# Pre-norm transposes reordered from token-major to feature-major, and the variance-row copies alternated between ScalarE and VectorE

## The reference, cut to what matters

```python
def _layernorm(x, axis=-1, eps=1e-5):
    m = jnp.mean(x, axis=axis, keepdims=True)
    v = jnp.var(x, axis=axis, keepdims=True)
    return (x - m) / jnp.sqrt(v + eps)

# x: (16, 2048, 1024); every sub-block is x + LN(f(LN(x)))
x = x + _layernorm(_L0_attn_ref(_layernorm(x), Wq, Wk, Wv, Wo))
x = x + _layernorm(_L0_ffn_ref(_layernorm(x), W_r, W_k, W_v, mu_r, mu_k))
x = x + _layernorm(_L1_attn_ref(_layernorm(x), W_attn, W_k2, W_proj))
x = x + _layernorm(_L1_ffn_ref(_layernorm(x), weights, scale, bias))

# _L0_attn_ref: 16 heads of 64; scores are a covariance plus a product of variances
qc = q - q.mean(axis=-1, keepdims=True)
kc = k - k.mean(axis=-1, keepdims=True)
cov = jnp.einsum('bhsd,bhtd->bhst', qc, kc) / D
q_var = jnp.var(q, axis=-1, ddof=1)
k_var = jnp.var(k, axis=-1, ddof=1)
scores = cov + q_var[..., :, None] * k_var[..., None, :] / D
out = softmax(scores) @ v          # then @ Wo
```

## Time and profile before

| | |
|---|---|
| median of 2 timed runs | 8365.75 us (8329.44 to 8402.06) |
| the profiled execution | 8285.25 us |
| its span on the slowest core (core 0) | 8283.6 us |
| spans of the other cores | 8252.1 to 8271.4 us |
| PE busy | 5208.9 us (63%) |
| DVE busy | 2943.7 us (36%) |
| ACT busy | 2610.7 us (32%) |
| PE, ACT, DVE on the chain that ended last | 44%, 10%, 22% |

### The profile page before, as it was taken

The page is one execution under the profiler, slowest core; times in us unless marked ns, Lnnn a source line. Parts: engine busy times, 40 slices in busy tenths (PEclk is TensorE's granted clock), DMA queues, the critical chain, the costliest instruction groups (busy, mean ns, idle before and its releaser), DMA issues.

```text
span 8283.6 us, 87354 instructions; the slowest of 8 cores (8252.1 to 8283.6 us)
## 1 busy us (share of the span) xinstructions
PE 5208.9 (63%) x27152; PEld 2902.5 (35%) x27392; DVE 2943.7 (36%) x4961; ACT 2610.7 (32%) x2875; POOL 375.8 (5%) x580
## 2 busy tenths in 40 slices
PE   4777777486466566654447777774865656666644
PEld 2444444233233333332124444442322333333321
DVE  3333332423433333335433333325134333333344
ACT  2443444110333333331024444441103333333310
POOL 0000000000000000000100000000000000000000
PEclk9777777698666666656667767766986666666566
DMA  2222222112122221111222222221121222111112
GB/s 36 18 18 22 21 18 15 13 16 21 5 12 12 14 12 11 7 10 11 52 32 18 18 25 18 18 17 11 16 21 5 12 13 13 11 11 7 10 11 49
DMA packets 244294, 140.02 MB, mean 17 GB/s; under 512 B 210946, under 2 KB 211074, under 8 KB 243842
## 3 DMA queue, kind: packets, MB, share of 16 engines
q1 hardware_dynamic: 21634, 33.72, 11.7%
q0 software_dynamic: 222208, 100.70, 9.1%
HBM read 117.59 MB, written 16.78 MB: 16 GB/s over the span
## 4 chain that ended last, share of the span: by engine, by line
PE 44%; DVE 22%; DMA 14%; ACT 10%; issue 9%; DVEq 1%; ACTq 0%; POOL 0%; SPq 0%; POOLq 0%
PE ps L114 24%; DMA TF<-TF 12%; PE psa L114 11%; PE psb L114 10%; ACT BCb L114 7%; DVE TF L114 7%; DVE STT L114 4%; DVE TBF L114 2%; DVE CH L114 2%; DVE WP L114 2%; ACT XT L114 1%; DVE XN L114 1%; DVE ODD L114 1%; DVEq L109 1%; DVE MV L114 1%
## 5 line engine op out<-in xcount | busy, mean ns | idle before, releaser
L114 ACT ACTIVATE BCb<-psa 128x1024 bf16<-128x1024 f32 (+1 forms) x1088 | 1059.1, 973 | 2297.0 <-PE psb L114 2177.0
L114 PE MATMUL ps<-BCb,VST 128*65 128x256 bf16 x6400 | 1262.9, 380 | 342.3 <-DVE BCb L114 319.4
L114 PEld LDWEIGHTS ps<-BCb,VST 128*65 128x65 bf16 x6400 | 1004.6, 161 | 596.8 <-issue 427.0
L114 DVE RECIPROCAL TF<-ps 1x512 f32<-1x512 f32 x256 | 858.0, 3352 | 958.7 <-PE psa L114 478.1
L114 ACT ACTIVATE BCb<-psb 128x1024 bf16<-128x1024 f32 (+1 forms) x1088 | 1054.7, 969 | 78.9 <-PE psb L114 62.0
L114 PE MATMUL ps<-XN,WP 128*128 128x512 bf16 x2936 | 861.3, 454 | 131.5 <-DVE CH L114 81.8
L114 PE MATMUL ps<-IDENTB,BA 128*128 128x128 bf16 x1024 | 129.4, 306 | 800.2 <-ACT BA L114 679.1
L114 PEld LDWEIGHTS ps<-XN,WP 128*128 128x128 bf16 x3072 | 344.8, 114 | 605.7 <-issue 406.9
L114 ACT ACT_TABLE_LOAD x43 | 55.2, 1283 | 1536.3 <-DVE SCR L114 845.2
L114 PE MATMUL psa<-QST,KST 65*128 65x256 bf16 x2048 | 369.3, 311 | 239.5 <-ACT BCb L114 190.5
L114 PE MATMUL psa<-XN,WP 128*128 128x512 bf16 (+1 forms) x1250 | 407.2, 408 | 126.6 <-DVE WP L114 108.3
(11 more groups left out here) (106 smaller groups left out, 5344.7 us busy)
## 6 DMA issues: line engine op xcount, KB each, us to landing
TF<-TF SPq DMA_DIRECT2D x256, 128.0 KB, 6.2
out<-X POOLq DMA_DIRECT2D x32, 512.0 KB, 5.6
X<-x POOLq DMA_DIRECT2D x32, 256.0 KB, 15.5
WP<-Wk POOLq DMA_DIRECT2D x32, 256.0 KB, 5.0
QST<-CH POOLq DMA_DIRECT2D x32, 256.0 KB, 2.9
KST<-CH POOLq DMA_DIRECT2D x32, 256.0 KB, 2.9
WP<-Wattn POOLq DMA_DIRECT2D x32, 256.0 KB, 4.7
WP<-Wq POOLq DMA_DIRECT2D x16, 256.0 KB, 4.5
```

Of the source, the lines that this page charges most:

```text
L114: instr = getattr(obj, rec["f"])(*rec["a"], **rec["k"])
```

## The change

Two edits.

1. `pre_ln`: the ACT normalisations stay in a loop over the 16 token tiles. The transposes and copies move out of it into a second loop, over the 8 feature chunks and, in each, two groups of 8 token tiles. A group transposes the block (tile, chunk) of 8 tiles into `PT`, and the copy moves the bank of 128x1024 to 1024 adjacent columns of one chunk of `XN`, and marks only that chunk as written. Counts and sizes of the ACT, PE and DVE instructions are as before (16 ACT, 128 transposes, 16 copies in each `pre_ln`).
2. `mk_sqvar`: the evacuations with even k stay on ACT, those with odd k become a DVE `tensor_copy` from the same bank to the same place. Banks, matmuls and DMAs are unchanged.

```diff
+            tiles = []
             for tt in range(TT):
...
+                tiles.append((dst_ap, dst_res))
                 b.op("s", "activation", dst_ap, X.t[:, tt * 1024: tt * 1024 + D],
...
-                ngrp = -(-C // 8)
-                for gi in range(ngrp):
-                    cs = list(range(gi * 8, min(C, gi * 8 + 8)))
-                    for k, c2 in enumerate(cs):
+            for c2 in range(C):
+                for g in range(-(-TT // 8)):
+                    ts = list(range(g * 8, min(TT, g * 8 + 8)))
+                    for k, tt in enumerate(ts):
+                        dst_ap, dst_res = tiles[tt]
                         b.op("t", "matmul", PT.t[:, k * 128:(k + 1) * 128],
                              dst_ap[:, c2 * 128:(c2 + 1) * 128], ident_ap,
-                             is_transpose=True, start=(k == 0), stop=(k == len(cs) - 1),
+                             is_transpose=True, start=(k == 0), stop=(k == len(ts) - 1),
                              r=list(dst_res) + IDENT.res, w=PT.res)
                     b.op("v", "tensor_copy",
-                         XNv[:, gi * 8: gi * 8 + len(cs), tt * 128: tt * 128 + 128],
-                         PT.t[:, 0: len(cs) * 128].rearrange("p (c j) -> p c j", c=len(cs)),
-                         r=PT.res, w=XN.res[gi * 8: gi * 8 + len(cs)])
+                         XN.t[:, c2 * T + g * 1024: c2 * T + g * 1024 + len(ts) * 128],
+                         PT.t[:, 0: len(ts) * 128],
+                         r=PT.res, w=XN.res[c2:c2 + 1])
...
-                            b.op("s", "activation",
-                                 stage.t[0:1, hs * T + g * 512: hs * T + g * 512 + 512],
-                                 pb_.t[0:1, 0:512], ACT.Copy, r=pb_.res,
-                                 w=stage.res[hs:hs + 1])
+                            dst = stage.t[0:1, hs * T + g * 512: hs * T + g * 512 + 512]
+                            if k % 2 == 0:
+                                b.op("s", "activation", dst, pb_.t[0:1, 0:512],
+                                     ACT.Copy, r=pb_.res, w=stage.res[hs:hs + 1])
+                            else:
+                                b.op("v", "tensor_copy", dst, pb_.t[0:1, 0:512],
+                                     r=pb_.res, w=stage.res[hs:hs + 1])
```

## The result

| | before | after |
|---|---|---|
| median | 8311.55 us (29 runs) | 8414.09 us (30 runs) |
| lowest | 8263.74 us | 8373.22 us |
| ratio after to before | | 1.013, 95% interval 1.0102 to 1.0158 |

The changed kernel is slower by 1.3%: by the interval 84 to 131 us, and 109 us between the lowest times. Forecast was +140.

A forecast was written before the change was run, and what follows sets the result against it. No engine is full, so waits in two stretches with hardly any overlap, pre_ln and the variance rows, were taken to count. 114 + 26 = +140 us on 8339 gave 8479, say 8480; range 8385 to 8560 us.

The forecast's parts named there:

- second term: Variance stretches: alternating evacuations over ACT and DVE would cost about 1.65 us per pair of heads, 26 us in all.
- Edit 1, 14.26 us each: pre_ln: last copy starts at 47.23 instead of 32.97 us after ACT's start, 14.26 us longer each, 114 us for eight.
- Rival 2: pre_ln: transposes run at the upper clock, eight in 0.61 us, so only +95 us, 8434; chance 0.1.
- Edit 2 inside its stretch: Variance stretch: copies still wait in turn; k gains about 0.04 us, the square of k starts 1.7 us later.
- 2.4 us of slack: Variance stretch: psa scores at 324.19 were given 2.4 us of slack because the psb scores start at 326.56.
- Per pair 1.7 - 0.04, about 1.65; 16 pairs give 26 us: Variance stretches: the later square of k less the small gain for k, counted in full for every pair of heads.
- The dearer rival: Same mechanisms, dearer: hand-offs at 0.26 us or PE longer at 1.2 GHz; about 8509, up to 8530; chance 0.25.
- Rival 3: Variance stretch: evacuations really side by side, -1.0 us per pair, -16 in all; total +98 us, 8437; chance 0.06.
- Rival 4: After pre_ln: projection matmuls run in PE's idle time between transposes, so not slower, -18 us, about 8320; chance 0.04.
- centre of 8339: Whole kernel before: mean of its three executions, 8339 us, the base to which the forecast added 140 us.

The follow-up runs named there:

- e6: Kernel before, with the DVE square of k done twice in each variance stretch; median 8306 us, lowest 8267 us, ratio 1.001.
- e9: Kernel before, all evacuations still on ACT but each writing a Res of its own; median 8222 us, lowest 8216 us, ratio 0.990.
- e5: Kernel before, its pre_ln order kept, with two banks in turn for the transposes; median 8160 us, lowest 8151 us, ratio 0.983.
- e4: Kernel before with the new pre_ln order and two banks in turn for the transposes; median 8268 us, lowest 8245 us, ratio 0.996.
- e3b: Kernel before, evacuations split over ACT and DVE, each with its own Res, DMA waiting only for its head's four copies; median 8230 us, ratio 0.992.

## Why the prediction was right or wrong

- **The outcome.** Forecast was slower by 140 us and within 2%; it is slower by 109 and within 2%, inside the range of 8385 to 8560 us at 8414. The sum hit because edit 1 is most of it: its second term, 26 us, was wrong, and the range of 175 us was wide enough to hide that.
- **Edit 1, 14.26 us each: right, 13.68.** The second copy came at 18.79 (forecast 18.89), the fourteen behind it at 1.99 each (forecast 2.024). The difference in the period is a wait: copies to a chunk come in pairs now, and only the second of a pair waits for an earlier copy on its own engine. From the first of eight transposes to the copy it is 1.12 us for the first of a pair (84.81 to 85.93) and 1.19 for the second (86.76 to 87.95), where before all but the first copy had 1.18 to 1.19. A copy to adjacent columns is not quicker, as taken from the earlier trace rows. Rival 2, the upper clock, didn't come: the granted clock stayed 0.50, and the trains of eight at 1.01 us.
- **Edit 2 inside its stretch: right in kind.** Copies of one head in turn, hand-offs of 0.1, 0.68 us for the DVE copy (taken: 0.69), the k square 1.5 us later (forecast 1.7). The k train ends 5.62 us after its first matmul (forecast 5.83), because copies for different heads followed each other closer than I had reckoned, two in 1.06 us on ACT and two in 1.28 on DVE. So even inside the stretch the price was 1.2 us and not 1.65: KST's second DMA comes 14.5 us after the q square against 13.3. The 2.4 us of slack that I gave the first psa scores are their distance to the psb scores; the gap left on PE between them is 1.36. Nothing hung on the difference.
- **The step that failed is "Per pair 1.7 - 0.04, about 1.65; 16 pairs give 26 us".** Edit 2 alone measured 1 us by lowest times, and 5 beside edit 1 (8373 - 8368). The step took for granted that what sets the start of a pair sets its end. `e6` shows that it doesn't: 1.3 us more in the same place costs nothing. The dearer rival had the clock in it, but the wrong way round, as a penalty on each delay.
- **Rival 3, side by side, was priced at -16 for edit 2** and the waits were given as what excludes it. That was right for this code, and taking the waits away made the copies go side by side, but the price was wrong by the same step: the stretch gained 1.6 us, the period 3.4, in all -47, and copies on ACT alone gained as much (`e9`).
- **Rival 4** was rightly given little: nothing of the projections moved ahead (behind the second `pre_ln` the first of them starts 4 us after the last copy starts).
- Both the failed step and the spread of the few runs of before that I had pushed the forecast up. Of the 66 us between 8480 and 8414, 37 are the change's own (140 against 102 between the medians), 27 the centre of 8339 that I gave the kernel before, whose median over 29 runs is 8312.

## What to carry to other kernels

Moving a loop out of another engine's loop takes its work out of that engine's shadow; reckon the new end from the shadow's end, then count how many turns stand behind it and what a turn costs with the buffers at hand. Here one more bank was worth 116 us in the old order and 123 in the new one, more than the order of the loops (100 and 94). When a dependency tracker has one object for several disjoint writes, splitting the writes over engines changes nothing but the length of each hand-off: free the object first, and see if the split is still needed. And before a local gain or loss is multiplied by the number of its places, put a dummy delay of the same size there and look at the period.

## What the runs showed of the hardware that I had not expected

- The time of a pair of heads is stepped. Shifts of the DMA that starts it by -1.8 to +4.0 us gave 163.8 to 163.9, 167.2 or 170.6 to 170.7 us, and the place at which PE's clock went from 1.2 to 2.4 GHz moved with them, from 25.5 to 28.9 and 32.3 us after the q square.
- Transposes alone can bring the clock up. In turn with the copies a whole `pre_ln` stayed at 0.50; with a second bank the later windows of the same stage read 1.00 and eight transposes took 0.61 us. These are the windows of `e5` (core 1) and `e4` (core 5), when PE had done nothing but transposes since the layer norm's statistics:

```profile
1628.00:1636.00 8.00, 4.30 (x60) 3.28 (x57) 4.84 (x7) 7.30 (x7) 0.00 (x0) 1.00 0.00 0
```
```profile
1652.00:1659.00 7.00, 4.88 (x66) 3.70 (x64) 5.44 (x9) 0.00 (x0) 0.00 (x0) 1.00 0.00 0
```

  The Trainium skill says in "TensorE: Matmul & The Clock Gate", section "Part 4: PE-mode transpose", that the full clock doesn't engage for transposes; these rows differ, and the measurement decides.
- A wait that is already met isn't free: about 0.06 us each on POOL (128 of them, 8.1 us, gone in `e3b`, which leaves them out), and 0.07 on DVE, where a copy with a wait on its own engine starts 1.19 us after the first of its transposes and one without 1.12.
